# Layer 0's projections start on an x turned in memory, batch 1's splits go to ScalarE and GpSimd, and the ternary comparisons move from the front into the attention groups

## The chip, the core and the metric

The kernel runs on one core of a Trainium2 chip. Its five engines each work through a list of their own, in order: PE (TensorE, matmuls), DVE (VectorE), ACT (ScalarE), POOL (GpSimd) and SP (SyncE, which here only issues DMAs). They wait for each other on semaphores. The metric is the device time of one execution in microseconds, the median of several runs.

## What is computed

Two post-norm transformer layers on x of shape 2 x 1024 x 256 (2048 tokens), float32. Layer 0 is causal attention with 16 heads of 16 and a feed-forward part with ternary weights; layer 1 is another attention and feed-forward.

```python
x = _layernorm(x + _L0_attn_ref(x, ...))   # qkv = x @ w_qkv; causal softmax(q k / 4) v; @ w_out + b_out
x = _layernorm(x + _L0_ffn_ref(x, ...))    # silu(x @ wu) * (x @ wg) @ wd, each w = ternary_quant(w)
x = _layernorm(x + _L1_attn_ref(x, ...))
x = _layernorm(x + _L1_ffn_ref(x, ...))
def ternary_quant(w): scale = mean(|w|) + 1e-8; return clip(round(w / scale), -1, 1) * scale
```

The ternary value of a weight is (w > 0.5 scale) minus (w < -0.5 scale); its scale is multiplied in later.

## The kernel before, in words

**The order of work.** Each engine walks through the same list of steps and does what is its own in it. For each layer there is an "opening" (`opening_of`), which computes q, k and v from x, and then eight groups (`plan`; `plan_by_table` in layer 0), each for 4 heads of one batch. The list is the order of issue: an engine that has to wait in one step does nothing of the steps behind it.

**The opening of layer 0.** x is loaded in four pieces of 512 tokens. A "turn" step lets PE transpose half a piece (4 transposes of 128x128) into a PSUM bank (line 698), and ACT or DVE copies it into the tile `xt` (lines 534 and 645; the profile calls it `prob`, whose memory it shares). A "unit" step is a projection of 512 tokens to 128 rows of q or k (2 matmuls in the program, 4 in the trace, line 727); there are 16 of them, 0 to 7 for batch 0, 8 to 15 for batch 1. A "v" step projects 256 tokens to v (line 707); there are 8. The scores are computed in bfloat16, so q and k are split into three bfloat16 parts: ACT writes part 1 (line 557), DVE the rest, the value minus part 1, into `staging` (line 654), ACT part 2 (line 586, the step "finish"), and DVE part 3, the rest minus part 2 (line 592); for batch 1 part 3 is POOL's (line 599). Parts 1 to 3 lie in the last of three buffers of the tiles `qop` and `kop`, in a ring of four. SP sends each unit's three parts to DRAM (line 504, 384 KB) and, when units 0 to 3 are there, loads the operands of group 0 back in the layout that scores need (lines 768 and 778, 12 DMAs). Operands of group 1 (the same 4 units) are loaded later, those of group 2 when all 16 units are sent.

**Maxima.** For every head and every 128 queries there is a "max" step: PE computes the scores (line 1181) into PSUM banks 0 to 3 and DVE takes the row maximum (line 1080). There are 32 in a group, 128 to 1024 columns wide, 12 score pieces a head. At most a few fit in the four banks, so PE waits for DVE (`max_done`) and DVE for PE. When a group's 32 maxima are done, "parts" and "rows" turn them into one row which SP sends into `qop` (lines 1095, 1255, 1103, 887). Only then can the group's "exp" steps begin, in which PE computes shifted scores (line 1195) and ACT the exponential. The maxima of group 0 stand in the opening, those of each later group among the exp steps of the group before it. `PE_SHARE` and `width` in `opening_of` spread the projections of batch 1 among the 32 maxima.

**The ternary weights.** POOL issues the loads of the three raw matrices (line 971, 1 MB each) when the first 1024 tokens of x are there. ACT sums their magnitudes (line 576, 128x2048 each), PE adds over the partitions (line 734), DVE makes thresholds and compares (lines 669 and 672, 128x2048, three times each).

## Time and profile before

| | us |
|---|---|
| median of 3 runs | 1007.37 (1007.07 to 1007.87) |
| the profiled execution, device time | 1006.18 |
| its span, first to last instruction | 1004.5 |
| PE busy | 950.5 (95%) |
| DVE busy | 690.4 (69%) |
| ACT busy | 593.1 (59%) |
| POOL busy | 354.1 (35%) |

The span is what the views of the trace cover; the device time is 1.7 us longer. A row of a timeline gives start, duration, engine, line, operation, tiles and count, and in brackets how long the engine was idle before it and what released it. "PEq", "SPq" and the like are an engine's queue, which issues DMAs.

### The profile page before, as it was taken

The page shows a single profiled execution, that of the slowest core. Times are in us where ns is not written, and L with a number is a line of the kernel's source. Part 1 is how long each engine was busy: PE and PEld are TensorE (multiplying, and loading weights), DVE is VectorE, ACT ScalarE, POOL GpSimd, SP SyncE. Part 2 cuts the span into 40 slices and gives each one's busy share as a digit, 9 for nine tenths or more (in the row PEclk, how much of TensorE's full clock was granted, in tenths as well). Part 3 has the DMA queues.
Part 4 walks back from the last instruction along what each step waited for, and adds up shares of the span by engine and source line. Part 5 has one row for each costly group of instructions (what it writes and reads, how often), then busy time and mean ns, then how long its engine had stood idle before and what let it go on. Part 6 is the DMA issues. An engine that isn't in the chain of part 4 may idle for free. (4 is left out here: it accounts for less than half of the span.)

```text
span 1004.5 us, 18031 instructions
## 1 busy us (share of the span) xinstructions
PE 950.5 (95%) x6546; PEld 516.3 (51%) x6546; DVE 690.4 (69%) x1529; ACT 593.1 (59%) x1210; POOL 354.1 (35%) x424
## 2 busy tenths in 40 slices
PE   6798999999998999988899999999999998999997
PEld 4453333333344887664334344343434354798896
DVE  2778888888843687578888888888888632433423
ACT  3434777777766345436577777777777767222321
POOL 3022123321222455234446354352615333323432
PEclk9798999999999999999799999999999999999999
DMA  7644111222000200152705142130401000000001
GB/s 245 198 157 123 48 39 43 65 64 64 2 2 15 81 1 8 45 176 55 221 2 177 29 150 84 53 118 19 136 1 40 2 1 1 1 1 22 22 1 42
DMA packets 32996, 64.20 MB, mean 64 GB/s; under 512 B 6095, under 2 KB 22367, under 8 KB 30532
## 3 DMA queue, kind: packets, MB, share of 16 engines
q1 hardware_dynamic: 31564, 58.47, 18.9%
q0 software_dynamic: 1072, 3.80, 1.1%
q8 instruction: 52, 0.85, 0.4%
q10 hardware_dynamic: 272, 0.79, 0.2%
q14 instruction: 36, 0.29, 0.1%
HBM read 50.45 MB, written 12.32 MB: 62 GB/s over the span
## 5 line engine op out<-in xcount | busy, mean ns | idle before, releaser
L1150 ACT ACTIVATE prob<-ps 128x512 f32<-128x512 f32 (+6 forms) x896 | 426.9, 541 | 158.9 <-PE ps L1195 155.9
L1195 PE MATMUL ps<-qop,kop 98*128 98x512 bf16 (+14 forms) x1376 | 271.4, 288 | 1.7 <-ACT prob L1150 0.6
L1181 PE MATMUL ps<-kop,qop 96*128 96x512 bf16 (+3 forms) x896 | 245.2, 359 | 14.8 <-DVE maxes L1080 11.2
L1195 PEld LDWEIGHTS ps<-qop,kop 107*128 107x128 bf16 (+1 forms) x1376 | 113.3, 97 | 212.8 <-ACT prob L1150 118.8
L1224 PE MATMUL ps<-prob,vst 128*32 128x512 f32 (+4 forms) x1792 | 211.2, 543 | 4.7 <-POOL prob L1017 2.9
L1080 DVE CUSTOM_DVE_ANT_0 sums<-ps,tri 128x128 bf16<-128x128 f32 (+7 forms) x256 | 180.6, 754 | 20.5 <-PE ps L1181 18.9
L1017 POOL TENSOR_TENSOR prob<-prob,keep 128x384 int32<-128x384 int32 (+2 forms) x144 | 121.7, 854 | 190.4 <-ACT prob L1150 189.9
L1080 DVE CUSTOM_DVE_ANT_0 sums<-ps,table 128x960 bf16<-128x960 f32 x128 | 148.0, 1156 | 48.2 <-PE ps L1181 35.9
L1625 PE MATMUL ps<-xs,wffn 128*128 128x512 f32 x640 | 156.1, 396 | 1.0 <-PEq L829 1.0
L1080 DVE CUSTOM_DVE_ANT_0 tri<-ps,table 128x960 bf16<-128x960 f32 x128 | 147.6, 1153 | 3.0 <-PE ps L1181 2.9
L1520 POOL TENSOR_TENSOR hs<-hf,hs 128x512 fp32r<-128x512 f32 x64 | 83.0, 1297 | 150.6 <-ACT hs L1543 142.3
L1625 PEld LDWEIGHTS ps<-xs,wffn 128*128 128x128 f32 x640 | 118.0, 188 | 27.8 <-issue 3.4
L1181 PEld LDWEIGHTS ps<-kop,qop 96*128 96x128 bf16 x896 | 79.5, 99 | 77.7 <-DVE maxes L1080 32.2
L1011 POOL TENSOR_SCALAR_AFFINE_SELECT prob<-prob 128x512 f32<-128x512 f32 x64 | 40.8, 638 | 166.1 <-ACT prob L1150 166.0
L1645 PE MATMUL ps<-wffn,hs 128*128 128x256 f32 x640 | 80.7, 284 | 0.6 <-POOL hs L1520 0.6
L1645 PEld LDWEIGHTS ps<-wffn,hs 128*128 128x128 f32 x640 | 78.8, 191 | 2.8 <-POOL hs L1520 1.0
L1585 DVE SCALAR_TENSOR_TENSOR hf<-ps,sg 128x512 f32<-128x512 f32 x32 | 22.1, 692 | 69.9 <-PE ps L1625 67.5
L1224 PEld LDWEIGHTS ps<-prob,vst 128*32 128x32 f32 x1792 | 36.1, 108 | 65.9 <-ACT prob L1150 43.6
L1543 ACT CAST hs<-hf 128x512 fp32r<-128x512 f32 x64 | 39.2, 613 | 44.8 <-PE ps L1645 41.3
L1551 ACT ACTIVATE sg<-ps 128x512 f32<-128x512 f32 x32 | 19.2, 598 | 69.1 <-PE ps L1625 69.1
L1080 DVE DVE_READ_ACCUMULATOR2_ANT maxes<- 128x1 f32 x512 | 42.5, 83 | 0.0
L727 PE MATMUL ps<-prob,w 128*128 128x512 f32 x80 | 39.8, 631 | 2.0 <-DVE staging L654 2.0
(106 smaller groups left out, 693.0 us busy)
## 6 DMA issues: line engine op xcount, KB each, us to landing
table<-in_table SPq DMA_DIRECT2D x32, 464.0 KB, 4.5
qop<-q_parts SPq DMA_DIRECT2D x96, 128.0 KB, 2.6
kop<-k_parts SPq DMA_DIRECT2D x48, 128.0 KB, 2.6
kop<-k_parts SPq DMA_DIRECT2D x48, 96.0 KB
q_parts<-qop SPq DMA_DIRECT2D x8, 384.0 KB, 3.8
q_parts<-kop SPq DMA_DIRECT2D x8, 384.0 KB, 2.6
x<-in_x SPq DMA_DIRECT2D x4, 512.0 KB, 6.1
k_parts<-qop SPq DMA_DIRECT2D x4, 384.0 KB, 2.7
```

The source lines that it names most:

```text
L727: last = nc.tensor.matmul(ps[:, self.bank(what, k), :], w[:, half, m * P:(m + 1) * P], src[:, half, t0:t0 + CH], start=(half == 0), stop=( ...
L1011: nc.gpsimd.affine_select(out=cells, in_=cells, pattern=[[0, HG], [1, P]], compare_op=ALU.is_ge, fill=zero, base=0, channel_multiplier=-1) ...
L1017: nc.gpsimd.tensor_tensor(bits, bits, keep[0:rows, off:off + b - a].unsqueeze(1) .to_broadcast((rows, MH, b - a)), ALU.mult).then_inc(mask ...
L1080: nc.vector.tensor_tensor_reduce(out=sums[k % 2][:, lo:hi], in0=scores, in1=mask, scale=1.0, scalar=LOWEST, op0=ALU.add, op1=ALU.max, accu ...
L1150: nc.scalar.activation(prob[0:rows, q % 2, k % HG, lo % CH:lo % CH + hi - lo], ps[0:rows, home["exp", n, k], lo % CH:lo % CH + hi - lo], A ...
L1181: last = nc.tensor.matmul(ps[:, S_BANK + score_slot(L, k)[0] + a // CH, a % CH:a % CH + b - a], qop[0:RD, par, h, i0:i0 + P], kop[0:RD, pa ...
L1195: return nc.tensor.matmul(ps[:, bank, a % CH:a % CH + b - a], lhs, rhs, start=start, stop=True, skip_group_check=True)
L1224: last = nc.tensor.matmul(ps[32 * h:32 * h + 32, O_BANK, lo % CH:lo % CH + hi - lo], vst[:, par, vt_, h % v_heads, :], prob[:, qd % 2, h, ...
L1520: nc.gpsimd.tensor_tensor(self.hidden(e, 1), hf[:, u % 2, :], self.hidden(e, 0).bitcast(F32), ALU.subtract).then_inc(self.h_lo, 1)
L1543: self.nc.scalar.copy(self.hidden(e, 0), self.K.hf[:, u % 2, :]).then_inc(self.h_hi, 1)
L1625: last = nc.tensor.matmul(ps[:, 2 * (u % 2) + which, :], weights[a][:, k, e * P:(e + 1) * P], prep.xs[:, c % 2, b, k, :], start=(n == 0), ...
L1645: last = nc.tensor.matmul(self.K.ps[:, 4 + half, (j % 2) * D:(j % 2 + 1) * D], self.hidden(e, b)[:, j * P:(j + 1) * P], self.wdown[a][:, e ...
```

## The change

The input x is also handed over transposed (`xt`, 256 x 2048). SP loads its four pieces straight into the tile `xt`, so layer 0 has no "turn" steps; the plain x, which only the residual needs, is loaded after the operands of group 2. The opening begins with units 0 to 3 and has their "finish" steps ahead of the first v. Projections use four PSUM banks (4 to 7) in the place of three. For units 8 to 15 ACT now writes a full float32 copy of the projection into `staging` behind part 1 (line 570 of the changed kernel), POOL subtracts part 1 from it (line 613) and later makes part 3 (line 603); DVE has no part in them. The raw weights are loaded when group 0's operands have landed, the magnitudes are summed by ACT among batch 1's units, and the thresholds are made behind the opening's "rows". The comparisons with the lower threshold are cut into 12 pieces of 512 columns and done by POOL in groups 0, 5 and 6 (line 621); the 12 others are done by DVE at the end of group 6 (line 681). Group 1's operands are loaded after unit 11 is sent, where that was after unit 9.

```diff
+BELOW_GROUPS, BELOW_QUADS = (0, N - 3, N - 2), (4, 5, 6, 7)
...
+        if group in BELOW_GROUPS and n in BELOW_QUADS:
+            steps.append(("below", 4 * BELOW_GROUPS.index(group) + BELOW_QUADS.index(n), 0))
+        if group == N - 2 and n >= nq - 4:
+            steps += [("ternary", 3 * (n - nq + 4) + k, 0) for k in range(3)]
...
-        first = proj.steps(0)
-        for j, step in enumerate((("unit", 2), ("unit", 4), ("v", 2))):
-            first.insert(first.index(step), ("abs", j))
-        at = first.index(("unit", 6))
-        first[at:at] = [("total", 0), ("threshold", 0), ("ternary", 0)]
-        first += [("ternary", 1), ("ternary", 2)]
-        out = [(what, k, 0) for what, k in first]
-
-    width = [hi - lo for _, _, lo, hi in units] if layer.index == 1 else [1] * len(units)
+        out = [(what, k, 0) for what, k in proj.steps(0)]
+
+    width = [hi - lo if layer.index == 1 else hi - lo + 2 * P for _, _, lo, hi in units]
     at = 3 if layer.index == 1 else 0
     out += [(what, k, 0) for what, k, _ in behind[:at]]
-    work, given = sum(share for _, _, share in behind[at:]), 0.0
+    last = len(behind) - (1 - layer.index)
+    work, given = sum(share for _, _, share in behind[at:last]), 0.0
     for n in range(len(units)):
         out.append(("max", n, 1))
         due = work * sum(width[:n + 1]) / sum(width[:-2])
-        if layer.index == 0:
-            due = -(-work * (n + 1) // (len(units) - 2))
         while at < len(behind) and given + behind[at][2] <= due + 1e-6:
             given += behind[at][2]
             out.append((*behind[at][:2], 0))
             at += 1
     out += [(what, k, 0) for what, k, _ in behind[at:]]
-    return out + [("parts", 0, 1), ("rows", 0, 1)] + [("max", k, 2) for k in range(AHEAD[layer.index])]
+    scale = [("total", 0, 0), ("threshold", 0, 0)] if layer.index == 0 else []
...
-            vs = [("v", v) for v in range(b * 4, b * 4 + 4)]
-            out = [*turns]
-            for j in range(4):
-                for _, u in units[2 * j:2 * j + 2]:
-                    out += [("unit", u), ("finish", u - 1)] if u >= 1 else [("unit", u)]
-                out.append(vs[j])
-            return out if b == 0 else out + [("finish", len(self.units) - 1)]
-        u, t, f = units, turns, [("finish", k) for _, k in units]
+            return [u[0], u[1], f[0], u[2], f[1], ("abs", 0), u[3], f[2], ("abs", 1), v[1], u[4], f[3], ("abs", 2),
+                    u[5], f[4], v[2], u[6], f[5], u[7], f[6], f[7], v[3]]
...
-        banks = ((4, 5, 6), (4, 5, 6)) if i == 0 else ((6, 7), (6, 7, 4, 5))
+        self.turns = [(c, s, k) for c in range(NC) for s in range(1 + i) for k in range(KD)] if i == 1 else []
+
+
+        banks = ((4, 5, 6, 7), (4, 5, 6, 7)) if i == 0 else ((6, 7), (6, 7, 4, 5))
...
-        return self.i == 1 and u >= self.half()
+        return u >= self.half()
...
+        elif what == "below":
+
+            j, cols, home = self.slice_of(k)
+            pool.wait_ge(self.tern, 3)
+            nc.gpsimd.tensor_scalar(self.below[:, home], self.raw[j][:, cols], self.thr[:, 1, j:j + 1], None, ALU.is_lt
+                                    ).then_inc(self.below_set, 1)
...
-            dve.wait_ge(self.tern, 3 + 2 * k)
-            nc.vector.tensor_scalar(self.below, self.raw[k], self.thr[:, 1, k:k + 1], None, ALU.is_lt
-                                    ).then_inc(self.tern, 1)
-            dve.wait_ge(self.tern, 4 + 2 * k)
-            nc.vector.scalar_tensor_tensor(out=K.wffn[:, k, 0, :], in0=self.raw[k], scalar=self.thr[:, 0, k:k + 1],
-                                           in1=self.below.bitcast(F32), op0=ALU.is_gt, op1=ALU.subtract
-                                           ).then_inc(self.tern, 1)
+            j, cols, home = self.slice_of(k)
+            dve.wait_ge(self.tern, 3)
+            dve.wait_ge(self.below_set, k + 1)
+            nc.vector.scalar_tensor_tensor(out=K.wffn[:, j, 0, cols], in0=self.raw[j][:, cols],
+                                           scalar=self.thr[:, 0, j:j + 1], in1=self.below[:, home],
+                                           op0=ALU.is_gt, op1=ALU.subtract).then_inc(self.tern, 1)
+
+    def slice_of(self, k):
+
+        parts = self.SLICES // 3
+        return k // parts, slice(k % parts * CH, (k % parts + 1) * CH), slice(k * CH, (k + 1) * CH)
...
+                def load_turned(c):
+                    sp.dma_start(proj.xt[c // 2][:, :, c % 2 * CH:(c % 2 + 1) * CH],
+                                 dram.xt.rearrange("(k p) t -> p k t", p=P)[:, :, c * CH:(c + 1) * CH]
+                                 ).then_inc(proj.x_loaded[c], 16)
+
+                for c in range(NC // 2):
+                    load_turned(c)
...
+                for c in range(NC // 2, NC):
+                    load_turned(c)
...
-            later = len(proj.units) // 2 + 2 * (1 - i)
+            later = len(proj.units) // 2 + 4 * (1 - i)
...
+                for c in range(NC):
+                    sp.dma_start(K.x[:, CT * c:CT * c + CT, :],
+                                 dram.x.rearrange("(t p) d -> p t d", p=P)[:, CT * c:CT * c + CT, :]
+                                 ).then_inc(proj.x_kept, 16)
...
+                pool.wait_ge(loaded[0], 16 * operands.loads)
+                for j, wt in enumerate(dram.ffn[0]):
+                    wt = wt.rearrange("(k p) n -> p k n", p=P)
+                    pool.dma_start(proj.raw[j].rearrange("p (k n) -> p k n", k=wt.shape[1]), wt
+                                   ).then_inc(proj.ffn_loaded, 16)
...
+        "x": a["L0_attn_x"].reshape(TOK, D), "xt": a["L0_attn_x"].reshape(TOK, D).T,
```

The first place is PE's list from its start. `w` and `prob` are the projection weights and the turned x, `kop` and `qop` the operands of scores. Before:

```order
L698 MATMUL ps<-ident,x 128x128 x16
L727 MATMUL ps<-prob,w 128x512 x4
L707 MATMUL ps<-w,prob 128x256 x4
L727 MATMUL ps<-prob,w 128x512 x4
L707 MATMUL ps<-w,prob 128x256 x4
L727 MATMUL ps<-prob,w 128x512 x4
L707 MATMUL ps<-w,prob 128x256 x4
L734 MATMUL ps<-wsum,ones 128x3
```

The same place after the change, up to the first scores (line 1206) and the first unit of batch 1:

```order
L741 MATMUL ps<-prob,w 128x512 x8
L718 MATMUL ps<-w,prob 128x256 x4
L741 MATMUL ps<-prob,w 128x512 x4
L718 MATMUL ps<-w,prob 128x256 x4
L741 MATMUL ps<-prob,w 128x512 x4
L718 MATMUL ps<-w,prob 128x256 x12
L1206 MATMUL ps<-kop,qop 128x128
L1206 MATMUL ps<-kop,qop 128x256
L1206 MATMUL ps<-kop,qop 128x384
L1206 MATMUL ps<-kop,qop 128x512 x2
L1206 MATMUL ps<-kop,qop 128x128
L741 MATMUL ps<-prob,w 128x512 x2
```

The transposes and the sum over magnitudes are gone, four units stand ahead of the first v, and a fifth v (batch 1's first) stands ahead of the scores.

The second place is POOL's list between its fills and the first causal mask. Before:

```order
L978 MEMSET mpart 128x128
L979 MEMSET vst 128x3072
L599 ISA
L599 TENSOR_TENSOR qop<-staging,qop 128x512 x2
L599 TENSOR_TENSOR kop<-staging,kop 128x512 x2
L599 TENSOR_TENSOR qop<-staging,qop 128x512 x2
L599 TENSOR_TENSOR kop<-staging,kop 128x512 x2
L990 COPY vst<-v_all 128x32x16
```

After, from the same fills to the end of unit 11 (what follows repeats the pattern up to unit 15):

```order
L994 MEMSET mpart 128x128
L995 MEMSET vst 128x3072
L1004 DMA raw<-in_up 128x2x1024
L1004 DMA raw<-in_gate 128x2x1024
L1004 DMA raw<-in_down 128x8x256
L613 ISA
L613 TENSOR_TENSOR staging<-staging,qop 128x512 x2
L603 TENSOR_TENSOR qop<-staging,qop 128x512
L613 TENSOR_TENSOR staging<-staging,kop 128x512
L603 TENSOR_TENSOR qop<-staging,qop 128x512
L613 TENSOR_TENSOR staging<-staging,kop 128x512
L603 TENSOR_TENSOR kop<-staging,kop 128x512
```

POOL has 16 differences in the place of 8, and the loads of the raw weights, with their wait for group 0's operands, stand in front of them.

The third place is DVE's list at the end of group 6, where the maxima of the last group are done; `attn` and `staging` belong to the preparation of the feed-forward part in group 7. Before:

```order
L1093 CAST mpart<-maxes 128x32
L1095 TENSOR_TENSOR mpart<-maxes,mpart 128x32
L1103 COPY mrow<-ps 128x128
L1357 COPY staging<-attn 128x1024
L1366 COPY staging<-ps 128x512 x2
```

After:

```order
L1118 CAST mpart<-maxes 128x32
L1120 TENSOR_TENSOR mpart<-maxes,mpart 128x32
L1128 COPY mrow<-ps 128x128
L681 SCALAR_TENSOR_TENSOR wffn<-raw,thr,below 128x512 x12
L1387 COPY staging<-attn 128x1024
L1396 COPY staging<-ps 128x512 x2
```

Twelve comparisons stand in front of the copy that PE's next transposes wait for.

## Rows read from the trace of the kernel before

**Rows 1.** The page: the span and the busy time of PE and others.

```profile
span 1004.5 us, 18031 instructions
PE 950.5 (95%) x6546; PEld 516.3 (51%) x6546; DVE 690.4 (69%) x1529; ACT 593.1 (59%) x1210; POOL 354.1 (35%) x424
```

**Rows 2.** Two stretches: start:end, length, PE, PEld, DVE, ACT, POOL, PEclk, DMA.

```profile
46.20:82.50 36.30, 32.83 (x116) 17.16 (x114) 28.20 (x74) 13.11 (x27) 9.79 (x9) 0.92 0.47 154
119.30:147.30 28.00, 27.93 (x203) 10.45 (x202) 24.37 (x72) 21.50 (x51) 8.43 (x14) 1.00 0.20 59
```

**Rows 3.** Timeline, the way to the first scores and maxima.

```profile
20.26 1.91 ACT L576 ACTIVATE xs<-raw 128x2048 fp32r<-128x2048 f32 x1 [3.21 <-DMA raw<-in_down]
28.54 0.36 SPq L504 DMA_DIRECT2D k_parts<-kop  x1
31.17 3.73 SPq L768 DMA_DIRECT2D qop<-q_parts  x6
41.00 0.22 PE L1181 MATMUL ps<-kop,qop 96*128 96x128 bf16 x1 [3.34 <-DMA kop<-k_parts]
43.92 2.35 DVE L672 SCALAR_TENSOR_TENSOR wffn<-raw,thr,xs 128x2048 fp32r<-128x2048 f32 x1
46.19 0.28 DVE L1080 CUSTOM_DVE_ANT_0 sums<-ps,tri 128x128 bf16<-128x128 f32 x1
```

**Rows 4.** Timeline of PE, projections of the opening.

```profile
10.78 3.85 PE L727 MATMUL ps<-prob,w 128*128 128x512 f32 x8
14.47 1.89 PE L707 MATMUL ps<-w,prob 128*128 128x256 f32 x8
16.20 3.60 PE L727 MATMUL ps<-prob,w 128*128 128x512 f32 x8
19.63 1.89 PE L707 MATMUL ps<-w,prob 128*128 128x256 f32 x8
23.52 5.40 PE L727 MATMUL ps<-prob,w 128*128 128x512 f32 x8 [2.00 <-DVE staging L654]
```

**Rows 5.** Timeline, unit 0 on its way through ACT, DVE and SP.

```profile
13.58 0.69 DVE L654 SCALAR_TENSOR_TENSOR staging<-ps,qop 128x512 f32<-128x512 f32 x1 [1.86 <-ACT qop L557]
15.16 0.61 ACT L586 CAST qop<-staging 128x512 bf16<-128x512 f32 x1
15.91 0.68 DVE L592 TENSOR_TENSOR qop<-staging,qop 128x512 bf16<-128x512 f32 x1
16.62 0.40 SPq L504 DMA_DIRECT2D q_parts<-qop  x1
```

**Rows 6.** DMA issues of 0 to 10 us: KB each, us to landing.

```profile
x<-in_x SPq DMA_DIRECT2D x2, 512.0 KB, 6.4
w<-in_w_qkv ACTq DMA_DIRECT2D x1, 768.0 KB, 4.9
```

**Rows 7.** 46.1 to 82.5 us: the maxima on DVE; PE's score pieces; POOL's differences.

```profile
46.10:82.50 36.40, 22.74 (x32) 0.92 0.48 155
...
59.45 0.87 PE L1181 MATMUL ps<-kop,qop 96*128 96x512 bf16 x4
...
L599 POOL TENSOR_TENSOR kop<-staging,kop 128x512 bf16<-128x512 f32 x4 | 4.6, 1156 | 6.6 <-ACT kop L586 6.6
```

**Rows 8.** Timeline, from the last send to the first exp step.

```profile
82.43 0.08 DVE L1080 DVE_READ_ACCUMULATOR2_ANT maxes<- 128x1 f32 x1
80.24 0.36 SPq L504 DMA_DIRECT2D k_parts<-kop  x1
83.59 1.17 SPq L887 DMA_DIRECT2D qop<-mrow  x2
86.32 0.58 PE L1195 MATMUL ps<-qop,kop 98*128 98x512 bf16 x1 [0.16 <-issue]
```

**Rows 9.** Timeline at the end of group 6, DVE and PE.

```profile
278.70 0.90 DVE L1357 COPY staging<-attn 128x1024 f32<-128x1024 f32 x1
287.84 1.09 PE L1434 MATMUL ps<-ident,staging 128*128 128x128 f32 x8
```

More of the change, by code:

```diff
@@ L240, in plan_by_table @@
     return steps
-PE_SHARE = ({"turn": 1, "unit": 1, "v": 1}, {"turn": 0.85, "unit": 1.72, "v": 1.72})
+PE_SHARE = ({"turn": 0.6, "unit": 1, "v": 1}, {"turn": 0.85, "unit": 1.72, "v": 1.72})
 def opening_of(layer, proj):
@@ L276, in opening_of @@
     out += [(what, k, 0) for what, k, _ in behind[at:]]
-    return out + [("parts", 0, 1), ("rows", 0, 1)] + [("max", k, 2) for k in range(AHEAD[layer.index])]
+    scale = [("total", 0, 0), ("threshold", 0, 0)] if layer.index == 0 else []
+    return out + [("parts", 0, 1), ("rows", 0, 1)] + scale + [("max", k, 2) for k in range(AHEAD[layer.index])]
 BRIDGE = {14: [("weigh", 0), ("decay", 0)],
@@ L320 @@
     SIDE = 7
-    STEPS = ("weigh", "decay", "divide", "scale", "turn", "unit", "finish", "v", "abs", "total", "threshold", "ternary")
+    TOTAL = 6
+    SLICES = 12
+    SET = 3 + SLICES
+    STEPS = ("weigh", "decay", "divide", "scale", "turn", "unit", "finish", "v", "abs", "total", "threshold", "below", "ternary")
     def __init__(self, nc, sem, K, L, dram, prep, before):
@@ L374, in __init__ @@
             self.v_units = list(range(B))
-        self.turns = [(c, s, k) for c in range(NC) for s in range(1 + i) for k in range(KD)]
-        banks = ((4, 5, 6), (4, 5, 6)) if i == 0 else ((6, 7), (6, 7, 4, 5))
+        self.turns = [(c, s, k) for c in range(NC) for s in range(1 + i) for k in range(KD)] if i == 1 else []
+        banks = ((4, 5, 6, 7), (4, 5, 6, 7)) if i == 0 else ((6, 7), (6, 7, 4, 5))
         self.bank_of, self.tenant, last_on = {}, {}, {}
@@ L575, in act @@
                 act.wait_ge(self.abs_sum, k)
-            nc.scalar.activation(self.below, self.raw[k], ACT.Abs, accum_out=self.wsum[:, k:k + 1]
+            nc.scalar.activation(self.magnitudes, self.raw[k], ACT.Abs, accum_out=self.wsum[:, k:k + 1]
                                  ).then_inc(self.abs_sum, 1)
@@ L1249, in step @@
                         pe.wait_ge(m_cut, n + 1)
[L1250 removed]
+                        if n == 0:
                             proj.wait_read(pe, *proj.last_on[SIDE])
@@ L1278, in step @@
                             pe.wait_ge(evicted, n * 2)
+                        elif k == 0 and i == 0:
+                            pe.wait_ge(proj.tern, 1)
                         pe.wait_ge(exp_done, n * NX + HG * (k + 1))
@@ L1284, in step @@
                     elif what == "norm":
+                        if i == 0 and n == 0 and k == 0:
+                            pe.wait_ge(proj.ident_loaded, 16)
                         pe.wait_ge(evicted, n * 2 + (k + 1))
@@ L1882 @@
     dram = Dram()
-    dram.x, dram.out = t["x"], out
+    dram.x, dram.xt, dram.out = t["x"], t["xt"], out
     dram.ident, dram.identb, dram.tri, dram.keep = t["ident"], t["identb"], t["tri"], t["keep"]
```

67 lines of the change are left out of this document (34 added, 33 removed).

## The prediction

> **What bounds the kernel now.** First the page: PE is busy for 95% of the span, DVE for 69% [rows 1]. Then busy time by stretch: in a group of layer 0's attention PE is busy 27.93 of 28.00 us at full clock [rows 2]. So nothing there is won by DVE, ACT or POOL, and a microsecond won ahead of it moves all that follows by a microsecond, as long as the same work stands behind. PE's slack lies in the opening, which is what the change rewrites; so I read its timelines from row to row and ask at each wait what ended last.
>
> The first chain runs to the first scores [rows 3]. ACT stands idle until 20.26 us for the raw weights, since the first magnitude sum stands in its list ahead of units 2 and 3. Unit 3 is therefore sent at 28.54, the operand loads start at 31.17 (2.63 us later) and the first score comes at 41.00 (9.83 us later). DVE is no earlier: it works at ternary comparisons until 46.19, the start of the first maximum. From there to the last maximum is a stretch of 36.30 us, with PE busy 32.83 and DVE 28.20 [rows 2]. The last maximum ends at about 82.5, the row is issued at 83.59, and the first exp step starts on PE at 86.32 [rows 8]. That last number is what I work out anew: behind it the lists hold the same PE work.
>
> **The start.** Before, PE starts when x has landed (6.4 us after its issue, the weights 4.9 us after theirs [rows 6]), transposes, and comes to unit 0 at 10.78 [rows 4]. The 32 transposes of both batches go, with their copies. Now unit 0 waits for the weights and the first piece of turned x, which is issued first of all. I take 6.5 us; the bounds are 6.2, from the weights, and 7.4, from x as it was.
>
> **PE up to the first scores.** Two units took 3.43 us (16.20 to 19.63) and a v 1.73 us (14.47 to 16.20) [rows 4]. Eight units and five v are 8 x 1.72 + 5 x 1.73 = 22.4 us. To this I add a slow beginning: the first pair of units took 3.69 us, against 3.43 for the second, although PE had already done 16 transposes; and a pair behind a wait of 2.00 us was busy 5.40 us, against 3.60 [rows 4]. With no transposes ahead, the units themselves are the first work. I take 1.7 us, near the 1.8 of the slow pair; the bounds are 0 and 1.8. PE is through at 6.5 + 22.4 + 1.7 = 30.6.
>
> [...]
>
> **The operands of group 0.** DVE's rest of unit 0 began 2.80 us after the unit did; cast to part 3 took 0.75 us and part 3 to the send 0.71 us [rows 5]. From rest to cast is 0.75 too (0.69 busy and a handover). Unit 3 is PE's fourth with nothing ahead of it, so its rest starts at 6.5 + 1.7 + 2.80 + 3 x 1.72 = 16.2, and its send at 16.2 + 0.75 + 0.75 + 0.71 = 18.4, in the place of 28.54. With the same 2.63 and 9.83 us the first score comes at 18.4 + 12.5 = 30.9, just behind PE's 30.6. Both paths meet here, so neither alone could be shortened. The raw weights wait for this load, so their 3 MB stay out of its way; DVE has only the splits of batch 0 in front and is free. The first maximum starts at about 31.2 in the place of 46.19: **15.0 us**. Of this the three comparison pairs on DVE would have been in the way (43.92 is the third of them [rows 3]).
>
> **The stretch of 32 maxima.** DVE loses eight rests there and keeps the maxima, 22.74 us busy with their overlaps [rows 7]. PE keeps 8 units (13.8), 3 v (5.2) and 48 score pieces; four of these filled 0.70 us behind 59.45 [rows 7], so 8.4 us. PE's sum is 27.4 us, with 1.2 us for the last maximum on DVE behind it and no v in that tail: it is PE-bound where it was held by both. Waits remain, because only two large maxima fit in the banks and three of them can stand between two projections: one takes DVE 0.71 us in the mean (22.74 / 32) and PE 0.26 (8.4 / 32), so a third of them waits about 0.5 us, the widest more, which happens in three or four places. I walked the two lists side by side with these durations and came to 29.4 us (27.5 to 31.5). The same walk over the list of before gives the trace's times to 0.3 us, apart from 2.5 us at half clock near 50 us. The last maximum ends at 30.9 + 29.4 = 60.3, in the place of 82.5. The stretch is worth 36.3 - 29.4 = 6.9 us, of which I lose some below.
>
> In the stretch ACT has 8 x 1.5 us of splits, three magnitude sums of 1.92 and v copies, 20 of 29 us; it waits for the raw weights (before, x had landed near 8 [rows 6] and they, behind it, by 20.26 [rows 3]; 12 us again gives 43), which is when it comes to the first sum. Cost 0; if they are 4 us late, ACT's delay reaches unit 12 and costs 2 to 3 us.
>
> **From the last maximum to the first exp.** This was 82.5 to 86.32, with the last send long over at 80.24 [rows 8]. Now unit 15 ends only some 2.8 us ahead of the last maximum's end, and behind it come two copies on ACT, POOL's 1.16 [rows 7], a cast, POOL's 1.16 again and a send, 4.9 us together. SP issues the row behind that send, at 60.3 + 2.3 = 62.6, instead of 1.1 us behind the last maximum, and it shares the queues with two fresh sends of 384 KB: 1.2 + 0.5 us. The second operand load, now behind unit 11's send at about 52, lands at about 62, when group 1's first scores want it: up to 0.6 us, beside the wait for the row. The first exp starts at 62.6 + 2.73 + 0.5 = 65.8. Gain: 86.3 - 65.8 = **20.5 us**.
>
> **Behind it.** POOL's 12 comparisons stand in quads without a causal mask, where it is idle, and cost nothing (bounds 0 and 0.5 each, since no row has this form). The 12 on DVE stand ahead of a copy that started at 278.70 and was wanted by PE at 287.84 [rows 9], 8.2 us of slack behind its own 0.90. A 512-column operation is busy 0.68 on DVE [rows 5], twelve of them at most 8.2: I take 0 and keep 0.5 as bound. The plain x (2 MB) is loaded behind group 2's operands and read in group 1.
>
> **Sum.** 1006.18 - 20.5 = 985.7 for an execution like the profiled one, which lay 1.19 below the median of 1007.37; against the median, 986.9.
>
> **Rivals.** *The cover collides.* Raw weights, operand load 1 and the sends meet between 42 and 62 us: if the raw loads take 20 us in the place of 12, ACT's sum waits 9 us, units 12 to 15 wait for banks, and 5 to 9 of the 20.5 us go: 991 to 995. For it speaks that ACT stood idle 3.21 us for just this load [rows 3]; against it, that the queues are busy for under half of 46 to 82 us (share 0.47 [rows 2]).
>
> *A warm start and fewer waits.* If PE's first units run at full rate and the small maxima leave it no gap, 1.7 + 1.9 us more: 983.3.
>
> *The stretch gives nothing.* If maxima and projections hold each other up as before, 36.3 us stay, 13.6 us remain: 993.8. Against it speaks DVE's idle time for the rests, which goes with them.
>
> *Slower than before: POOL's differences are the bound.* Each unit of batch 1 now needs POOL twice before its parts are whole, and PE's bank and SP's send wait behind ACT, which waits for POOL. At 1.16 us this is 18.5 us of POOL in 29 [rows 7]. To turn 20.5 us of gain into 2 of loss, 16 of them would have to take 22.5 us more, 2.6 us each, with the whole surplus on the path. The row shows 1.16 in the mean beside DVE's maxima. It would give 1009 or more.
>
> [...]
>
> **How the numbers follow.** Forecast as summed, 984.5 to 989.5: 0.57. Collision of the cover: 0.15. The stretch gives little: 0.10. The warm start, 982 to 984.5: 0.12. No gain, because group 0 gives it back: 0.02. Slower by POOL: 0.04. The range for 8 in 10 takes the forecast, the warm start and the near half of the two losses: 982 to 993. About 0.2% (2 us) is what a measurement of this kernel can tell from no change: faster 0.94, same 0.02, slower 0.04.
>
> **What would show it.** PE's first unit at 6.2 to 7.4 us, its first pair near 5 us long; the fourth send at about 18.4; the first score at about 31 with PE idle under 0.5 us ahead; 32 maxima in 28 to 31 us with PE idle for about 2; the row issued right behind unit 15's send; the first exp near 66; the last group's first transposes as many us earlier as the first exp. The prediction is wrong if ACT's first magnitude sum waits several us, if POOL's differences grow beyond 1.2 us, if the clock falls while PE waits for the first operands, or if PE turns up idle behind the twelve comparisons on DVE.

## The result, and the profile after

The changed kernel takes 996.00 us (median of 4 runs, 995.53 to 996.74) beside 1007.62 us for the kernel before on the same chip (1007.07 to 1008.41): ratio 0.9885, interval 0.9868 to 0.9902. That is 11.6 us faster, where 20.5 us were forecast, and 3 us above the range. A second set of runs, on another chip, gave 995.63 (ratio 0.9886).

The profiled execution after has a device time of 996.74 us. Its page, as [rows 1]:

```profile
span 995.0 us, 18001 instructions
PE 944.1 (95%) x6514; PEld 510.5 (51%) x6514; DVE 685.0 (69%) x1525; ACT 593.2 (60%) x1212; POOL 382.1 (38%) x444
```

PE still has 95% of the span. So the comparison goes by marks, as the prediction did. The way to the first maximum, from the timeline (it answers to [rows 3, 4]), and the stretch of maxima by window (as the first of [rows 2]):

```profile
8.14 9.93 PE L741 MATMUL ps<-prob,w 128*128 128x512 f32 x16 [8.14 <-DMA w<-in_w_qkv]
...
20.83 0.36 SPq L508 DMA_DIRECT2D k_parts<-kop  x1
23.83 3.73 SPq L783 DMA_DIRECT2D qop<-q_parts  x6
...
33.40 0.71 PE L1206 MATMUL ps<-kop,qop 96*128 96x128 bf16 x4
33.78 0.29 DVE L1105 CUSTOM_DVE_ANT_0 sums<-ps,tri 128x128 bf16<-128x128 f32 x1 [1.74 <-PE ps L1206]
```

```profile
33.70:62.90 29.20, 27.42 (x103) 13.99 (x100) 22.69 (x65) 19.24 (x35) 16.71 (x16) 1.00 0.69 230
```

PE starts at 8.14 instead of 6.5, its first four units take 9.76 us (the next line begins at 17.90), and the first maximum comes at 33.78 instead of 31.2. The stretch itself is 29.05 us, close to the forecast 29.4, with PE busy 27.42 (worked out: 27.4) at full clock. Now the second half, where most was lost: ACT, SP, DVE, POOL and PE of the timeline, in the order of the argument.

```profile
48.34 1.91 ACT L580 ACTIVATE xs<-raw 128x2048 fp32r<-128x2048 f32 x1 [5.28 <-DMA raw<-in_down]
...
53.76 0.36 SPq L508 DMA_DIRECT2D q_parts<-kop  x1
57.68 0.36 SPq L508 DMA_DIRECT2D k_parts<-kop  x1
58.09 3.66 SPq L783 DMA_DIRECT2D qop<-q_parts  x6
61.79 3.75 SPq L793 DMA_DIRECT2D kop<-k_parts  x6
65.64 0.53 SPq L508 DMA_DIRECT2D q_parts<-qop  x1
...
67.58 0.98 SPq L508 DMA_DIRECT2D k_parts<-kop  x1
68.61 2.48 SPq L902 DMA_DIRECT2D qop<-mrow  x2
...
62.75 0.08 DVE L1105 DVE_READ_ACCUMULATOR2_ANT maxes<- 128x1 f32 x1
...
58.76 1.16 POOL L613 TENSOR_TENSOR staging<-staging,qop 128x512 f32<-128x512 f32 x1 [1.11 <-ACT staging L570]
...
64.34 2.26 POOL L603 TENSOR_TENSOR kop<-staging,kop 128x512 bf16<-128x512 f32 x2
...
65.72 0.26 PE L1280 MATMUL ps<-identb,mpart 128*128 128x128 bf16 x1 [3.01 <-ACT v_all L547]
...
72.74 0.58 PE L1220 MATMUL ps<-qop,kop 98*128 98x512 bf16 x1 [1.96 <-DMA qop<-mrow]
```

Read it downwards. ACT waits 5.28 us for the raw weights, so units 10 and 11 are sent at 53.76 and 57.68. SP holds the second operand load behind unit 11's send, and its twelve issues occupy SP until 65.5. Units 12 to 15 and then the row stand behind them: the row goes out at 68.61, 5.8 us behind the last maximum, which ends at 62.83 (forecast 2.3). SP's queue is not all of that: POOL runs seven differences without a gap from 58.76 to 66.60, so unit 15 could not have been sent before 66.60, and the row not before 67.0. So 1.6 us of the lateness is the queue's, and the rest is that of ACT and POOL. PE's row of 65.72 shows that the transposition of the maxima waited for ACT's copy of v, not for DVE. The row of 68.61 shows that its two issues take 2.48 us where [rows 8] had 1.17, and it lands late too. The first exp step is at 72.74 (forecast 65.8; in the kernel before 86.32): a gain of 13.6 us.

The issues of 0 to 36 us, with KB each and median us to landing (as [rows 6]):

```profile
raw<-in_up POOLq DMA_DIRECT2D x1, 1024.0 KB, 7.6
...
raw<-in_down POOLq DMA_DIRECT2D x1, 1024.0 KB, 13.1
w<-in_w_qkv ACTq DMA_DIRECT2D x1, 768.0 KB, 7.3
```

And the end of group 6 (as [rows 9]):

```profile
265.72 9.70 DVE L681 SCALAR_TENSOR_TENSOR wffn<-raw,thr,below 128x512 fp32r<-128x512 f32 x12
276.07 1.09 PE L1464 MATMUL ps<-ident,staging 128*128 128x128 f32 x8 [0.66 <-DVE staging L1387]
```

The twelve comparisons take 9.70 us, not 8.2 at most, and PE waits 0.66 us behind them. At the first normalisation 11.8 us of gain are left and stay to the end of layer 0. In layer 1's opening, whose list is the same in both kernels, this execution loses 2.4 us more.

### The profile page after: what moved, and what is told of

Read it like the earlier page. It is cut to its first block and busy times, and to the rows that moved or that the text cites. A ratio compares the mean times of both kernels' runs of the same rounds, so it can differ in the third digit from the quotient of the medians.

```text
span 995.0 us, 18001 instructions
## 1 busy us (share of the span) xinstructions
PE 944.1 (95%) x6514; PEld 510.5 (51%) x6514; DVE 685.0 (69%) x1525; ACT 593.2 (60%) x1212; POOL 382.1 (38%) x444
```

## The experiments

Each run has its marks in one table: the fourth send, operand load 0, the first score on PE, the row's issue, the first exp step on PE, all in us; then the gain at layer 0's first normalisation, against the first profile of the kernel before; then the median time. There are four sets of runs (e1 to e4, e5 to e8, e9 to e12, e13 to e15), each with its own runs of the kernel before (medians 1006.17, 1006.96, 1006.58 and 1006.79). Runs of one kernel scatter by up to 6 us there, so marks decide where medians are close; each mark is from one execution. e11's time is that of a single execution.

| run | send | load 0 | score | row | exp | gain | median |
|---|---|---|---|---|---|---|---|
| changed | 20.83 | 23.83 | 33.40 | 68.61 | 72.74 | 11.8 | 996.00 |
| e1 raw early | 19.72 | 28.25 | 37.88 | 71.56 | 74.34 | 10.4 | 996.23 |
| e2 load 1 sooner | 20.55 | 23.56 | 33.22 | 66.81 | 69.76 | 13.6 | 993.95 |
| e3 comparisons behind | 19.48 | 22.48 | 32.25 | 66.50 | 70.51 | 14.9 | 994.23 |
| e4 warmed | 17.96 | 22.75 | 33.39 | 67.14 | 72.89 | 9.8 | 996.00 |
| e5 own count | 20.07 | 23.07 | 32.91 | 64.94 | 68.75 | 14.6 | 991.61 |
| e6 differences on DVE | 19.30 | 22.31 | 32.17 | 74.93 | 77.66 | 5.6 | 1001.91 |
| e7 pieces behind w | 20.42 | 23.42 | 33.18 | 68.03 | 72.04 | 12.5 | 996.61 |
| e8 five edits | 17.83 | 22.83 | 32.84 | 66.08 | 70.45 | 15.6 | 993.47 |
| e9 = e5 and e3 | 19.32 | 22.32 | 32.12 | 64.15 | 66.92 | 18.6 | 990.51 |
| e10 changed again | 19.36 | 22.36 | 31.93 | 67.30 | 71.29 | 12.3 | 995.63 |
| e11 before again | 28.84 | 31.47 | 40.97 | 82.06 | 85.55 | -0.4 | 1008.54 |
| e12 one piece with w | 18.25 | 24.20 | 33.81 | 67.77 | 71.87 | 12.6 | 996.03 |
| e13 warmed, loads moved | 17.95 | 20.96 | 31.77 | 63.81 | 69.02 | 16.4 | 991.70 |
| e14 warmed, on e9 | 17.86 | 21.33 | 32.02 | 65.75 | 70.01 | 16.1 | 991.82 |
| e15 last two on DVE | 20.49 | 23.50 | 33.17 | 64.99 | 69.05 | 16.2 | 991.56 |

### e1: the raw weights early

In the POOL block:

```diff
                 pool.wait_ge(proj.x_loaded[1], 16)
+                for j, wt in enumerate(dram.ffn[0]):
...
-            if i == 0:
-                pool.wait_ge(loaded[0], 16 * operands.loads)
-                for j, wt in enumerate(dram.ffn[0]):
...
```

> The three raw weight loads of layer 0's feed-forward are issued behind the second piece of x, and no longer behind the landing of the first operand load. Theory A (the late raw landing at 48.3 us, for which ScalarE waited 5.28 us, is what made the maxima-to-first-exponential stretch 9.9 us long instead of 5.5): the wait goes, units 10 and 11 are sent about 5 us sooner, operand load 1 is issued near 53 us, and the first exponential comes at 67 to 69 us instead of 72.7; time 991 to 993 us against 996.0. Theory B (the loads then share the queues with the sends of units 0 to 3 and with the first operand load): the first score slips by 1 to 3 us from 33.4 and eats the gain, 995 to 998 us. Theory C (raw's lateness is hidden by the order on SP anyway): first score and first exponential stay, 996 us.

Theory B held for the start, and more of it than it gave. The timeline of PE and of ACT:

```profile
37.88 0.70 PE L1204 MATMUL ps<-kop,qop 96*128 96x128 bf16 x4 [4.06 <-DMA kop<-k_parts]
49.08 1.92 ACT L580 ACTIVATE xs<-raw 128x2048 fp32r<-128x2048 f32 x1
```

ACT no longer waits, but load 0 goes out 8.5 us behind the fourth send instead of 3.0, and PE waits 4.06 us for it: beside the raw weights the four sends take 8.2 to 9.7 us to land, in the changed kernel 2.5 to 2.9. Of the 4.5 us lost there, the first exp gets 2.9 back. So the change's order (raw behind the first operands) is right, and still the raw weights' lateness has a price.

### e2: operand load 1 behind unit 9

```diff
-            later = len(proj.units) // 2 + 4 * (1 - i)
+            later = len(proj.units) // 2 + 2 * (1 - i)
```

> SP issues operand load 1 behind the send of unit 9 instead of unit 11. Theory A' (what is late is SP's queue: load 1 at 58.1 us holds the sends of units 12 to 15 and then the row back until 68.6 us): load 1 goes out near 46 us, the sends of units 12 to 15 go out as their third parts are done, by 66.6 us, TensorE's first scores of group 1 no longer wait for it, and the row is issued at 66.3 to 67 us (behind the copied maxima): first exponential 70.5 to 71.5 us, time 994 to 995 us. Rival (the row waits for the maxima's copy, which is late because ScalarE and GpSimd are, and not for SP): at most 0.5 us comes off, 995.5 to 996 us. With it, units 10 and 11 keep their dates of 53.8 and 57.7 us, since ScalarE's wait for the raw weights stays.

Theory A' held: load 1 at 45.21, the sends of units 12 to 15 by 66.39, and units 10 and 11 unmoved.

```profile
45.21 3.75 SPq L783 DMA_DIRECT2D qop<-q_parts  x6
66.81 1.18 SPq L902 DMA_DIRECT2D qop<-mrow  x2
```

The row leaves 1.8 us sooner and also flies faster: its issues take 1.18 us, and the exp step follows 2.95 us behind instead of 4.13. The first exp gains 3.0 us. But the row still leaves 4.2 us behind the last maximum (62.63), since unit 15's send goes out right behind POOL's last difference, which ends at 66.37. ACT's wait for the raw weights is untouched here, and with it POOL's lateness.

### e3: the comparisons behind a gather

```diff
-        if group == N - 2 and n >= nq - 4:
-            steps += [("ternary", 3 * (n - nq + 4) + k, 0) for k in range(3)]
...
+    if nq == 12:
+        at[2][1:1] = [("ternary", k) for k in range(12)]
```

> VectorE's 12 comparisons stand behind the first gather of group 7 instead of ahead of it. Theory (the 9.7 us of them stand on the path, because TensorE's feed-forward then waits for VectorE's copy, 0.66 us, and the gain falls from 12.8 to 11.8 us there): 1.0 us comes off, 994.8 to 995.3 us. Rival (they only move the wait: the weights are then late for the feed-forward's first matmuls, or the 9.7 us stand ahead of another copy): 996 to 999 us.

The theory held by the marks. Between group 6 and the first normalisation the gain falls by 0.3 us instead of 1.0. The rest of this run's lead is its start, 1.15 us sooner at the first score: its first four units took 8.59 us instead of 9.76, which the edit does not touch.

### e4: TensorE warmed

```diff
+            if i == 0:
+                pe.wait_ge(proj.ones_set, 1)
+                for _ in range(16):
+                    nc.tensor.matmul(ps[:, 0, 0:P], K.ones[:], K.ones[:], start=True, stop=True)
             if before is not None:
                 before.pe(pe)
```

> TensorE runs 16 small matmuls on the constant ones ahead of the first unit, while it waits for the weights anyway; nothing of the result changes. Theory (the first matmuls ran at 1061 to 1224 ns instead of 592 because the clock had been low before them, at a price of 2.9 us): the first four units take 7 us instead of 9.76, the first score comes 1.5 to 2.9 us sooner, time 993 to 994.5 us. Rival (16 small ones are too few or end too early, and the clock is low again by then): nothing changes, 996 us. Second rival (they end after the weights land and hold the units up): the first unit starts after 8.14 us, time up to 997 us.

None of the three as written; the time is the first rival's, for another reason. The units take 7.0 us and the fourth send is out at 17.96, but the first score is where it was. PE and SP of the timeline:

```profile
8.06 7.13 PE L741 MATMUL ps<-prob,w 128*128 128x512 f32 x16 [1.69 <-DMA w<-in_w_qkv]
22.75 4.65 SPq L783 DMA_DIRECT2D qop<-q_parts  x6
33.39 0.70 PE L1206 MATMUL ps<-kop,qop 96*128 96x128 bf16 x4 [2.69 <-DMA kop<-k_parts]
```

The 2.8 us won on PE come back as a wait for the operands: load 0 leaves 4.8 us behind the fourth send. e13 and e14 take that up.

### e5: a count of its own for the first raw load

```diff
-        self.ffn_loaded = sem("ffn_loaded0") if i == 0 else None
+        self.ffn_loaded = [sem(f"ffn_loaded0_{j}") for j in range(2)] if i == 0 else None
...
-            act.wait_ge(self.ffn_loaded, 16 * 3)
+            act.wait_ge(self.ffn_loaded[min(k, 1)], 16 * (1 + min(k, 1)))
```

The semaphore for it is freed by letting the third and fourth piece of x share one.

> The three raw weight loads keep their place, but the first has a semaphore of its own, so that ScalarE's first absolute sum waits for it alone (issued at 33.8 us, it lands at 41.4 us) and no longer for the last of the three at 48.3 us. Theory A (ScalarE's 5.28 us wait is what delays units 10 and 11, operand load 1 and the row): the wait at 43.1 us is gone, units 10 and 11 are sent near 49 and 53 us, operand load 1 goes out near 53.5 us, the sends of units 12 to 15 behind it by 66 us, the row at 66.5 us, and the first exponential comes near 70.5 us instead of 73.4: 2.5 to 3.5 us off, 992.5 to 993.5 us where the changed kernel has 996. Rival (the backlog only moves: the second sum then waits for the last load, and units 12 to 15 come at the rate of ScalarE and GpSimd): under 0.7 us off.

Theory A held, and the median is 1 us better than it gave (runs from 988.84 to 993.57). No transfer moved; one wait did:

```profile
42.45 1.92 ACT L580 ACTIVATE xs<-raw 128x2048 fp32r<-128x2048 f32 x1
47.76 1.91 ACT L580 ACTIVATE xs<-raw 128x2048 fp32r<-128x2048 f32 x1 [1.81 <-DMA raw<-in_down]
68.75 0.59 PE L1220 MATMUL ps<-qop,kop 98*128 98x512 bf16 x1 [0.88 <-DMA qop<-mrow]
```

With the first score 0.5 us sooner, the first exp is 4.0 us sooner: 3.5 us for the wait. The row now leaves 2.6 us behind the last maximum (62.33). Later 2.6 us of it go again at the comparisons, where the granted clock fell (0.71 in the mean of 270 to 274 us; in the changed kernel's first profile it stayed at 1.00).

### e6: batch 1's differences back on DVE

```diff
     def off_dve(self, u):
-        return u >= self.half()
+        return self.i == 1 and u >= self.half()
```

> Batch 1's differences in layer 0 go back to VectorE (one operation from PSUM instead of ScalarE's full copy and GpSimd's subtraction); the rest of the change stays. If the change's third part pays: the stretch between the first and the last maximum is longer than its 29.05 us, by up to the 8 x 0.69 us that VectorE has more, 2 to 5.5 us, and the time is 998 to 1001 us. Rival (the differences did nothing but move work onto ScalarE and GpSimd, whose backlog makes the 9.9 us behind the last maximum): the stretch grows by 1 to 3 us, but the last maximum is followed by the first exponential within 7 us, and the time is 994 to 997 us.

The change's third part pays, by more than either theory gave. The window of the maxima, then DVE and PE of the timeline:

```profile
32.50:73.60 41.10, 30.14 (x102) 14.60 (x100) 27.41 (x73) 16.62 (x29) 11.60 (x12) 0.92 0.62 203
```

```profile
49.74 0.69 DVE L664 SCALAR_TENSOR_TENSOR staging<-ps,kop 128x512 f32<-128x512 f32 x1 [5.74 <-ACT kop L561]
51.36 1.04 PE L1206 MATMUL ps<-kop,qop 96*128 96x512 bf16 x2 [6.75 <-DVE maxes L1105]
```

The stretch grows from 29 to 41 us. With DVE in the chain, ACT's wait for the raw weights stops DVE for 5.74 us, DVE's maxima stop PE for 6.75, and the granted clock falls (0.92 in the mean of the stretch). The differences on ACT and POOL took work off DVE and also kept ACT's wait away from PE. How much each of the two is worth is not shown; this edit was not run without ACT's wait. Behind the last maximum the exp step then follows in some 4 us, as before.

### e7 and e12: fewer bytes beside the weights

e7 makes SP wait for the weights ahead of the third piece of x; e12 does so ahead of the second.

```diff
+                sp.wait_ge(proj.w_loaded, 16)
                 for c in range(NC // 2, NC):
                     load_turned(c)
```

> SP issues the third and fourth piece of x only when the projection weights have landed. Theory (the weights took 7.3 us to land instead of 4.9 because 2 MB of x share the queues): the first unit starts near 7.0 us instead of 8.1; and since the two pieces then lie in the way of the first sends, load 0 comes no earlier than 2.9 us behind the send of unit 3. First score 1 us sooner if TensorE is still what sets it, time 995 us. Rival (the weights' own 0.77 MB behind 1 MB of the first pieces is what takes 7 us): the first unit stays within 0.3 us of 8.1 us and nothing is won; with the pieces in the way of the sends 0 to 2 us are lost.

> Only the first piece of x goes out with the projection weights; the second piece, the identity and the rest wait until the weights have landed. Theory (the weights land late because the bytes issued with them share the 16 engines: 1.3 MB instead of 1.85 and more): the weights land at 6 to 6.8 us and the first unit starts there, 1.3 to 2 us sooner; the second piece, needed for unit 2, lands near 11 to 12 us and costs little of it. Rival (what takes the time is the weights' own load): the first unit stays at 8 us, and unit 2 waits for the late second piece, 0 to 1 us lost; 996 to 997 us.

In e7 the rival held: the first unit stays at 8.04. In e12 the theory held for the weights (6.96, where it gave 6 to 6.8), and the gain was eaten. PE of e12:

```profile
6.96 8.53 PE L741 MATMUL ps<-prob,w 128*128 128x512 f32 x16 [6.96 <-DMA w<-in_w_qkv]
33.81 1.84 PE L1207 MATMUL ps<-kop,qop 96*128 96x128 bf16 x6 [2.83 <-DMA kop<-k_parts]
```

With the second piece and `ident` issued behind the weights (e12), the weights land after 6.1 us instead of 7.3; with only the third and fourth piece behind them (e7), after 7.2. The amount alone does not explain it: in the kernel before, 1 MB of x and `ident` were issued at the same time, and the weights landed after 4.9 us; here they take 7.3, and 6.1 in e12 with half a MB beside them. What makes the rest is open. The pieces then meet the first sends, and load 0 leaves 6.0 us behind the fourth.

### e8: five edits together

e2, e3, e4, e5 and e7 in one.

> Five edits together: the first raw load's own semaphore, operand load 1 behind unit 9's send, the comparisons behind the first gather of group 7, TensorE warmed, and the third and fourth piece of x behind the weights. By the sum of the parts (2.7 us for operand load 1's place as measured, 1 for the comparisons, 1.5 to 3 for the raw loads, 2 for a start that no longer meets the pieces of x on the queues): 987 to 990 us. Rival (the parts cure the same wait, and the warmed start stays bound by the landing of the first operand load at 33.4 us): 991 to 993 us.

The rival held in kind, 0.5 us above its band. Load 0 left 5.0 us behind the fourth send. Beside e5's own count, e2's edit only moved the burst: load 1 went out at 46.05 and held units 10 and 11 until 53.62 and 54.24 (47.88 and 53.72 in e5). The row left 33.2 us behind the first score, in e5 32.0.

### e9 to e11: the two that pay, and both kernels again

e9 is e5 and e3 together; e10 is the changed kernel and e11 the kernel before, unaltered.

> The two edits that paid alone, without the other three of the combination: the first raw load's own semaphore, and the comparisons behind the first gather of group 7. Theory (their gains add: the own semaphore brought the 17.2 us of gain that stand up to group 7, of which the comparisons ahead of the copy then took 2.7): the gain at the first normalisation is 16.5 to 17.2 us, the time 990 to 991.5 us. Rival (the clock falls again in group 7's end whatever the order, since TensorE waits there): 14.5 to 15 us of gain and 992 us.

> The changed kernel itself once more, with a second profile: a measure for the others of this call. If its first four units (9.9 us at first) and layer 1's low clock at 437 to 447 us are the kernel's own, both come again within 0.3 us; if they vary from one execution to the next, the four units take 8.6 to 9.9 us as in the other runs, and the gain lost in layer 1 differs from 2.4 us.

> The kernel before once more, for a second profile of it. Theory (layer 1's opening is the same list of instructions in both, and the kernel before was lucky in the clock there, low for 3.6 us only): its second profile shows the clock low for longer at 445 to 455 us and the span 1 to 2 us above 1004.5. Rival (the changed kernel really loses 2.4 us there, for its phase of the clock is another): the low stretch of the kernel before is the same as in its first profile, within 0.5 us.

e9's theory held, with a gain above it: 990.51 us (990.09 to 990.78; ratio 0.9837, 0.9823 to 0.9852), 5.1 us under the changed kernel beside it and the best version here. From the same first score as e10 (32.12 and 31.93) its exp step is 4.4 us sooner, at 66.92. DVE, SP and PE of e9:

```profile
61.46 0.08 DVE L1105 DVE_READ_ACCUMULATOR2_ANT maxes<- 128x1 f32 x1
...
64.15 1.18 SPq L902 DMA_DIRECT2D qop<-mrow  x2
...
66.92 0.59 PE L1220 MATMUL ps<-qop,kop 98*128 98x512 bf16 x1
```

With ACT's first sum no longer waiting (it starts at 41.67), the row leaves 2.6 us behind the last maximum (61.54) and the first exp comes 5.4 us behind it: 2.3 and 5.5 were forecast. At the comparisons e9 loses 0.2 us, and e10 2.6, its granted clock falling to 0.59 in 274 to 278 us.

e10 shows what is scatter: its first four units take 8.5 us, and layer 1 costs it 1.9 us, not 2.4. e11's theory held: the kernel before loses 1.9 us there against its own first profile. Layer 1's opening by window, the kernel before, then again, then the changed one:

```profile
436.00:461.00 25.00, 19.95 (x92) 11.53 (x91) 22.91 (x47) 8.58 (x20) 5.38 (x7) 0.93 0.39 122
```

```profile
437.00:462.00 25.00, 19.44 (x88) 10.57 (x87) 21.86 (x45) 6.80 (x15) 4.32 (x6) 0.86 0.38 118
```

```profile
424.00:449.00 25.00, 20.23 (x86) 11.19 (x85) 20.57 (x44) 6.43 (x13) 3.47 (x6) 0.80 0.38 114
```

The granted clock differs (0.93, 0.86, 0.80) for one list of instructions. So the profile that the prediction was made against was a lucky one by some 2 us in layer 1. Against it the runs of the changed lists lose between 0.2 (e1) and 2.6 us (e13) behind the first normalisation, and no run shows that any of it belongs to the change.

### e13 to e15: what holds the operands, and the small copies

e13 is e9 with e4's matmuls and POOL's loads of `keep` and the two biases moved behind the raw weights; e14 is e9 with e4's matmuls alone.

```diff
-                pool.dma_start(K.keep[:], dram.keep).then_inc(K.tri_loaded, 16)
-                for j in range(2):
-                    pool.dma_start(K.bias[:, j, :], dram.bias[j].to_broadcast((P, D))).then_inc(K.tri_loaded, 16)
...
+            if i == 0:
+                pool.wait_ge(K.tri_loaded, 16 * 2)
+                pool.dma_start(K.keep[:], dram.keep).then_inc(K.tri_loaded, 16)
...
```

> On the version of 990.5 us: TensorE warmed by 16 small matmuls, and GpSimd's loads of keep and of the two broadcast biases issued behind the raw weights instead of at 9 us. Theory (with TensorE warm the fourth send goes out at 18 us, but the first sends then meet GpSimd's five constant loads on the queues and take 4.5 to 5.8 us instead of 2.5 to 2.9, which ate the gain): the sends take 3 to 3.5 us, operand load 0 goes out at 21 to 21.5 us, the first score comes at 30.5 to 31.3 us, and 0.8 to 1.5 us come off: 989 to 989.8 us. Rival (the sends meet the last pieces of x, not those loads): operand load 0 stays at 22.5 us or later, the first score at 32 us, 990.5 us.

> The same with the warmed TensorE and no load moved. Theory: as in the first warmed run operand load 0 stays at 22.3 to 22.8 us, the first score at 32 to 33 us, and the time is that of the version without it, 990.5 us within 0.5. Rival (the earlier units help even so, since all of batch 0's projections end 2.9 us sooner): 989.5 us or less.

The landing of the four sends, issues of 9 to 24 us, in e4 and then in e13:

```profile
q_parts<-qop SPq DMA_DIRECT2D x1, 384.0 KB, 5.8
...
k_parts<-kop SPq DMA_DIRECT2D x1, 384.0 KB, 4.7
```

```profile
q_parts<-qop SPq DMA_DIRECT2D x1, 384.0 KB, 2.5
...
k_parts<-kop SPq DMA_DIRECT2D x1, 384.0 KB, 2.9
```

e13 against e14 shows the mechanism, though smaller than e4 made it look: with three of POOL's five loads out of the way (0.36 MB) load 0 follows the fourth send by 3.0 us again, at 20.96; in e14 by 3.5, its sends landing in 3.2 to 4.5 us. Neither paid in time (991.70 and 991.82, e9 in the set before 990.51), and both missed the time that was expected. The first score came at 31.77 and 32.02, since the six issues of load 0 took 4.9 and 4.6 us instead of 3.7; then the row flew 5.2 and 4.3 us. Why the issues are slower is open, and so is the row's flight, which over all runs went from 2.7 (e6) and 2.8 us (e9) to 5.8 us (e4).

e15 is e9 with units 14 and 15 exempt from `off_dve`.

```diff
-        return u >= self.half()
+        return u >= self.half() and not (self.i == 0 and u >= 14)
```

> On the version of 990.5 us: the differences of units 14 and 15 by VectorE from PSUM instead of ScalarE's full copy and GpSimd's subtraction. Theory (VectorE's two small copies of the maxima take 0.88 and 1.09 us instead of 0.18 and 0.19, since each ends only as GpSimd's running instruction does, and that is 1.6 us on the path): GpSimd is then done 1 to 2 us sooner, the two take under 0.8 us together, and the first exponential comes 0.5 to 1.2 us sooner although VectorE has 2 x 0.69 us more ahead of its last maxima; 989.5 to 990.5 us. Rival (the two differences wait on VectorE for their turn, and the last maxima come later by 1.4 us or more): 991 to 992.5 us.

It settles what stretches the small copies, and brings nothing. In the changed kernel POOL and DVE ran so:

```profile
62.12 1.15 POOL L603 TENSOR_TENSOR qop<-staging,qop 128x512 bf16<-128x512 f32 x1
63.23 1.15 POOL L613 TENSOR_TENSOR staging<-staging,kop 128x512 f32<-128x512 f32 x1
...
62.87 0.44 DVE L1118 CAST mpart<-maxes 128x32 bf16<-128x32 f32 x1
63.34 1.09 DVE L1120 TENSOR_TENSOR mpart<-maxes,mpart 128x32 bf16<-128x32 f32 x1
```

DVE's cast ends at 63.31 and its subtraction at 64.43, each 0.04 to 0.05 us behind POOL's instruction (63.27 and 64.38). In e15, with POOL's difference out of the way:

```profile
63.48 0.54 DVE L1122 CAST mpart<-maxes 128x32 bf16<-128x32 f32 x1
64.05 0.19 DVE L1124 TENSOR_TENSOR mpart<-maxes,mpart 128x32 bf16<-128x32 f32 x1
```

The pair takes 0.73 us instead of e9's 1.97, and the cast still ends 0.04 us behind a copy of POOL's (63.98). But DVE's two more rests push the last maximum back by 0.9 us, and the row is issued 31.8 us behind the first score instead of 32.0: 0.2 us, under what was expected. Nor was there more to win in e9: its row goes out at 64.15, and unit 15's send, which stands before it on SP, is over only at 63.91. The time, 991.56, lies in the rival's band, but 1.0 us of it is the later first score.

## Why the prediction was wrong

**The direction and the plan held.** ACT's and DVE's early waits went, and the stretch came out at 29.05 us for 29.4. PE in group 0 and on had the same work. From the first score, from which the prediction's sum counts it, the stretch was 29.43. Of the rivals, the cover's collision is what happened, at a smaller size: it took 20 us for the raw loads and a wait of 9, where 14.6 and 5.28 were measured. Its 991 to 995 took the start as forecast and was counted from the profiled execution; from the median it would be 992 to 996.

**The step that failed: "Cost 0" for ACT's first sum.** The prediction took 12 us for the raw loads and had them landed at 43. They took 14.6 us from a later issue (33.78) and landed at 48.3. They share the queues with the sends of units 4 to 9, 5.4 MB in 33 to 50 us at 318 GB/s. The wait also was not for the first load, landed at 41.4, but for the last of three on one semaphore. It was named as 2 to 3 us at 4 us late; at 5.28 us it was worth 3.5 (e5). That ACT's first sum would wait several us was one of the prediction's own signs of being wrong.

**From the last maximum to the first exp: 9.9 us, not 5.5.** That is in the main the same cause seen downstream: without ACT's wait it is 5.4 (e9). The prediction set the row behind unit 15's send, 2.3 us after the last maximum; it was 5.8. Of these 3.5 us, 1.9 are POOL, which got its work late and ended at 66.60, and 1.6 are SP's queue: the prediction did not see that load 1's twelve issues (7.4 us of SP) stand ahead of units 12 to 15 once unit 11 is late. e2 undoes the queue alone, for 3.0 us, 0.2 of it the start and 1.2 a faster flight of the row. Here e2 and e5 overlap. The flight was put at 3.2 us and was 4.1; why is open. Behind the gap the granted clock read 0.50 from 66 to 78 us, where the kernel before had 0.53 from 86 to 90 and 1.00 from 90 to 94; the gain fell from 13.6 us at the first exp to 12.8 at 84 us, 0.8 us more.

**The small copies.** The prediction gave no cost to POOL on this path. DVE's two copies took 1.53 us instead of 0.37 (0.18 and 0.19 before), in e5 and e9 1.97. Each of the stretched ones ended within 0.05 us of the end of the POOL instruction beside it (in the changed kernel and e15, above); at the end of group 6, with POOL idle, the same two took 0.18 and 0.19 us in the changed kernel too (264.85 and 265.06 us). What the prediction weighed, POOL's differences beside the maxima, indeed did not slow: a difference took 1.15 to 1.16 us and the widest maximum (128x1024) 1.22, in both kernels. The case it didn't look at was a copy between two SBUF tiles behind the maxima. The price here is small: in the changed kernel the transposition waited for ACT, beyond the end of the pair, and in e9 unit 15's send left 0.2 us to win.

**The start, 2.5 us late at the first score.** PE was through 2.8 us late, at 33.4 for 30.6, and the first score, put 0.3 us behind that, followed at once. Weights 1.6: PE started at 8.14 for 6.5, and 1.2 of it goes when the second piece of x and `ident` are issued later (e12). Slow beginning: the first four units took 9.76 us and, behind 16 small matmuls, 6.97, so 2.8 against 1.7 (upper bound 1.8); over the runs it is 1.4 to 2.8, so 1.1 of it may be scatter. The granted clock reads 1.00 in both cases, so no row shows that the clock is what made them slow. Neither term could be had alone: e4 and e12 removed one each, and the first score stayed (33.39 and 33.81), since the sends landed later. The prediction said that both paths meet; it did not price the meeting.

**The twelve comparisons.** Taken as 0 with a bound of 0.5, at 0.68 us each. They took 0.81 each: seven took 0.74, three of them in part beside one of POOL's masks, and the other five, all beside one, 0.90 to 1.12. Price: 1.0 us, and 2.6 where the granted clock fell with it (to 0.71 in 270 to 274 us of e5, to 0.59 in 274 to 278 of e10). In e3 and e9 it is 0.3 and 0.2.

**Sum.** 20.5, less 2.5 (start), 4.4 (row: 3.5 its issue, 0.9 its flight), 0.8 (clock behind the gap), 1.0 (comparisons) is 11.8, the gain in layer 0 and, within 0.2, that of the medians. e9's 18.6 us in layer 0, with a first score 1.3 us sooner, is what the change is worth without its two avoidable waits. The prediction's own steps add up to 20.2 rather than 20.5 us, since it counts the first maximum from 31.2 and the stretch from 30.9.

## What to carry to other kernels

Where one semaphore counts several loads and its reader waits for the whole count, the first reader waits for the last of them (here until 48.3 us, where the first load had landed at 41.4); give the first its own before moving anything. When a long DMA burst (here 7.4 us of SP) is tied to a send, ask what stands behind it on the same issuing queue if that send is late. Where two paths meet within 0.3 us, each needs a cure, and here the cure of one moved its transfers into those of the other (the first score stayed at 33.39 us in e4 and 33.81 in e12): measure edits together as well as alone.

## What the runs showed that was not expected

- DVE copies of 128 x 32 between SBUF tiles, 0.18 and 0.19 us alone, took up to 0.88 and 1.09 us, ending 0.04 to 0.05 us behind the POOL instruction beside them.
- Three small POOL loads (0.36 MB) stretched four 384 KB sends from 2.5 to 2.9 us (e13) to 3.2 to 4.5 us (e14), and in e4 they took 4.5 to 5.8.
- Two issues of 8 KB took SP 1.17 to 2.70 us. It was 1.18 in e2 and e9 too, with unit 15's send 0.6 us or less ahead; what makes the difference is open.
- The first 16 projection matmuls took 8.5 to 9.9 us and, behind 16 small matmuls, 7.1 us (busy time), while the clock column read 1.00 both times (changed kernel and e4).
- The same instructions in layer 1 ran at a mean granted clock of 0.80 to 0.93.
